# Sorted rows of 2112 bytes at a pitch of 2112, ScalarE's up parts behind the last norm, and idle transposes in TensorE's waits

## The chip, the cores and the metric

The kernel runs on one core of one Trainium2 chip. The metric is the device time of the whole kernel in microseconds (us): the median of three runs for the kernel before.

## What is computed

```python
x = x + jnp.tanh(g_xattn[0]) * _L0_xattn_ref(_layernorm(x), L0_xattn_k, fside_S2_0, ctx_2048, ctx_2048, 8)
x = x + jnp.tanh(g_ffn[0]) * _L0_ffn_ref(_layernorm(x), router_w, gate_w, up_w, down_w)
```

x is float32, 8 x 256 rows of 512. The first half is a gated long convolution: for every head (32 heads of 8 rows) the outer product kv of the normed rows and the context rows is convolved along the 512 positions with that head's filter k, a skip term is added, and the result is contracted with the context again. The second half is a mixture of experts with top-1 routing over 8 experts:

```python
routing_indices = jnp.argmax(einsum(hidden, router_w), axis=-1)
for e in range(8):
    y = (silu(hidden @ gate_w[e]) * (hidden @ up_w[e])) @ down_w[e]
    out = out + where(routing_indices == e, y, 0)
```

gate_w and up_w are 512 x 1024 for each expert, down_w is 1024 x 512.

## The kernel before, in words

The five engines and the DMA queues are programmed by hand in one block each; there is no scheduler. Every engine runs its own instructions in the order in which its block writes them, and semaphores (`wait_ge`, `then_inc`) tie them together. SyncE (SP) issues nearly all loads and stores, ScalarE (ACT) issues the loads of `xs`, and GpSimd (POOL) issues the indirect transfers.

**Attention part.** 16 groups g of 128 rows, two heads each. `stages` runs one stage per group on each engine, the middle ones in a loop. In a stage TensorE (PE) runs the convolution of group g (`conv`, 60 matmuls of 128x512 in float32r, each product taken as high times high, low times high and high times low part), the transposes of the normed rows of group g+2 (`v_in`), and for group g-1 the sum over heads (`sum_heads`) and the transposes of the second norm (`x2_in`), and for group g-2 the router's logits. VectorE (DVE) makes kv (`outer`, L962), multiplies the convolution's banks (`product`, L977), and does the residual and both norms' statistics. ScalarE takes the roots and norms and makes `kv_hi`; GpSimd makes `kv_lo` and adds products. SyncE also fills the DRAM tensor `sorted_x` in advance with rows that belong to nobody (`fill_rows`, 14 DMAs of 384 rows, written from a 128-row tile `fill`).

At the start TensorE transposes groups 0 and 1 (`v_in(0)`, `v_in(1)`), then begins stage 0. `v_in(1)` writes the bank from which VectorE makes the two products kv of group 0, so it waits for both (`s_kv`). VectorE waits for the two gates' tanh (ScalarE, L856 and L857) before its own stage 0.

**Hand-over.** Each token's normed row of 512 floats, and its number as the 513th, stands in `xn_all` in SBUF, group after group, 513 floats each. As soon as the places of groups 0 to 13 are known (`places_first`, semaphore `s_pos`), GpSimd writes those rows to their places in `sorted_x`, sorted by expert, with one indirect DMA of 128 rows per group (`scatter`, L431). The last two groups follow when the last norm, the last logits and `places_last` are done. A row of `sorted_x` is 513 floats, 2052 bytes, and so is its pitch. Meanwhile the first expert's weights are loaded in chunks of 512 KB through the one buffer `raw` (four chunks per matrix, L441) and split into high and low parts: for gate and up of expert 0 ScalarE makes the high part (`first_high_parts`, L456) and VectorE the low part (`first_low_parts`, L463). A chunk of up is loaded when the same chunk of gate has been split, a chunk of down when the same chunk of up has been. In ScalarE's order, the first two chunks of up stand ahead of the last group's root and norm (`root2(G - 1)`, L811 and L768):

```python
                xn2T_out(G - 2)
                logits_out(G - 2)
                act.wait_ge(s_y, G * 2 * LB)
                first_high_parts(act, UP, range(2))
                root2(G - 1)
                norm2(G - 1, 1)
```

**Expert part.** When all 16 scatters have landed (`s_scat`), ScalarE loads a tile of 128 sorted rows into `xs` (L878), TensorE transposes it (`x_in_array`, L1208), ScalarE and GpSimd make its high and low parts (L882, L884, L712), and TensorE runs gate and up (`project`, L1219, 24 matmuls each), the transposes of the next `xs`, `down` of the tile before (L1232, 24 matmuls) and the transposes of `hid` (L1252). In this run there are 19 such tiles, then `down` of the last tile alone, and its rows go out with an indirect DMA (L724). All later weights are split by VectorE alone (L1078, L1081). Tiles 0 and 1 belong to expert 0.

Of the kernel before, what the change touches and what calls it, by code (L numbers as in the profile page):

```python
# [5 lines left out]
def flamingo_layer_kernel(  # L6
# [30 lines left out]
    f32 = mybir.dt.float32  # L37
# [24 lines left out]
    KPAD = P + L  # L62
    CH = 4
# [6 lines left out]
    sorted_x = nc.dram_tensor("sorted_x", [FILL * (G - 2) * P, L + 1], f32)  # L70
# [6 lines left out]
    def put(name, shape, dt=f32, at=None):  # L77
        size = 4
        for n in shape[1:]:
            size *= n  # L80
        size = (size + 31) // 32 * 32
        if at is None:
            at = place
        t = nc.alloc_sbuf_tensor_at(name, shape, dt, offset=at[0])
        at[0] += size
        return t
# [37 lines left out]
    place[0] += 4 * G  # L124
# [26 lines left out]
    xn_all = put("xn_all", [P, G, L + 1], f32, [up_at + slot])  # L151
# [8 lines left out]
    assert up_at + slot + 4 * G * (L + 1) <= down_at  # L160
# [35 lines left out]
    fill = put("fill", [P, L + 1], f32, att)  # L196
# [7 lines left out]
    with ctx:  # L204
# [95 lines left out]
        def known(g, test):  # L300

            return test(g) if isinstance(g, int) else True
# [125 lines left out]
        def scatter(eng, groups):  # L428

            for g in groups:  # L430
                nc.gpsimd.indirect_dma_start(  # L431
                    out=sorted_x[:, :], out_offset=bass.IndirectOffsetOnAxis(ap=pos[:, g:g + 1], axis=0),
                    in_=xn_all[:, g, :], in_offset=None).then_inc(s_scat, 16)
# [73 lines left out]
        with nc.Block() as block:  # L507

            @block.sync
            def _(eng):  # L510
# [26 lines left out]
                def fill_rows(g):  # L537
                    eng.dma_start(sorted_x[blk(g - 1, FILL * P), :].rearrange("(k p) n -> p k n", p=P),
                                  fill[:, :].unsqueeze(1).broadcast_to([P, FILL, L + 1])).then_inc(s_zfill, 16)
# [62 lines left out]
            def _(eng):  # L602
                nc.gpsimd.memset(fill[:, 0:L], 0.0).then_inc(s_const, 1)
                nc.gpsimd.memset(fill[:, L:L + 1], float(NOBODY)).then_inc(s_const, 1)
# [24 lines left out]
                nc.gpsimd.memset(hot[:, G1:G + 1, :], 0.0).then_inc(s_const, 1)  # L629

# [64 lines left out]
                eng.wait_ge(s_xnc, G1)  # L695
# [66 lines left out]
            def _(act):  # L762
# [98 lines left out]
                act.wait_ge(s_y, G * 2 * LB)  # L861
                first_high_parts(act, UP, range(2))
# [6 lines left out]
                first_high_parts(act, UP, range(2, CH))  # L869

                def load(t):
                    if isinstance(t, int) and t == 0:
                        place = slice(0, P)
                    else:
                        act.wait_ge(s_next, t)
                        place = bass.ds(act.value_load(tile_at[0:1, blk(t)], min_val=0,
                                                       max_val=(FILL * (G - 2) - 1) * P), P)
                    act.dma_start(xs[:, :], sorted_x[place, :]).then_inc(s_xs, 16)  # L878
# [42 lines left out]
            def _(dve):  # L921
# [145 lines left out]
                first_low_parts(dve, UP, range(2))  # L1067
# [3 lines left out]
                first_low_parts(dve, UP, range(2, CH))  # L1071
# [36 lines left out]
            def _(pe):  # L1108
                def transposes(bank, src, done):
                    for b in range(LB):  # L1110
                        last = nc.tensor.transpose(bank[:, b * P:(b + 1) * P], src(slice(b * P, (b + 1) * P)),  # L1111
                                                   ident[:, :])
                    last.then_inc(done, 1)

# [56 lines left out]
                def stage(g, u, n):  # L1171
                    before = known(g, lambda g: g >= 1)
                    conv(g, u, n, 0, (0, 1, 2))
                    if known(g, lambda g: g >= 2):
                        logits_of(g - 2)
# [15 lines left out]
                v_in(1)  # L1191
# [63 lines left out]

                x_in_array(0)
                pe.wait_ge(s_tab, 1)
                last_tile = tiles(pe, tile)
                down(last_tile)
# [39 lines left out]
```

## Time and profile before

| what | value |
|---|---|
| median of 3 runs | 741.34 us (739.51 to 743.07) |
| the profiled execution's own time | 740.68 us |
| its span, first to last instruction | 738.8 us |
| busy: PE / DVE / ACT / POOL | 87% / 68% / 33% / 76% of the span |
| mean granted clock of TensorE | 0.938 of full speed |
| chain that ended last | PE 78%, DMA 7%, POOL 6%, DVE 4% |
| DMA | 117.8 MB, mean 159 GB/s |

PE, DVE, ACT and POOL stand for TensorE, VectorE, ScalarE and GpSimd. The span leaves out some 2 us ahead of and behind the instructions. The chain is followed back from the last instruction, at each step to what released it. The clock is what the chip granted TensorE: 1.00 is 2.4 GHz, 0.50 is 1.2 GHz. For the start of the program, up to 21.5 us, the trace holds no clock, and 1.00 is shown there.

### The profile page before, as it was taken

The numbers are of one execution on the slowest core, as the hardware profiler recorded it, in microseconds if no ns is written. First come the engines' busy times: TensorE is split into PE (matmuls) and PEld (weight loads), VectorE is DVE, ScalarE is ACT, GpSimd is POOL, SyncE is SP. The second block draws the span as 40 slices with busy tenths as digits, with TensorE's granted clock in tenths as the row PEclk, the third lists the DMA queues.
The fourth block names the chain that finished last, engine by engine and source line by source line (L and its number), as shares of the span: only waits on it lengthen the run. The fifth ranks groups of instructions, "written<-read, shape, count | busy, mean of one in ns | idle before, by whom it ended". The sixth has DMA issues, their size and how long they took to land.

```text
span 738.8 us, 10659 instructions
## 1 busy us (share of the span) xinstructions
PE 639.8 (87%) x3058; PEld 524.0 (71%) x3059; DVE 499.7 (68%) x631; ACT 241.7 (33%) x351; POOL 559.7 (76%) x361
## 2 busy tenths in 40 slices
PE   0989999999999999310379999999999999999964
PEld 0878888888888878310258888888888888888853
DVE  5678888888888897650746557599999938533200
ACT  4534333344334432220022332323333333333330
POOL 2799999999999998630224777798888878786852
PEclk9999999999999999655589999999999999999996
DMA  7156778677777763799864444466665655431110
GB/s 228 61 144 174 183 186 207 177 171 183 194 189 174 181 163 139 140 151 109 249 219 128 155 156 156 154 197 213 223 213 202 217 157 183 142 130 28 56 43 4
DMA packets 52031, 117.80 MB, mean 159 GB/s; under 512 B 5772, under 2 KB 5964, under 8 KB 52016
## 3 DMA queue, kind: packets, MB, share of 16 engines
q1 hardware_dynamic: 43712, 99.35, 49.0%
q0 software_dynamic: 4320, 12.60, 7.5%
q10 hardware_dynamic: 3984, 5.67, 2.7%
q8 instruction: 7, 0.11, 0.1%
q14 instruction: 8, 0.07, 0.0%
HBM read 94.60 MB, written 24.57 MB: 161 GB/s over the span
## 4 chain that ended last, share of the span: by engine, by line
PE 78%; DMA 7%; POOL 6%; DVE 4%; issue 3%; ACT 2%; SPq 0%; POOLq 0%; DVEq 0%; ACTq 0%
PE pair L1219 30%; PE bank L1131 23%; PE bank L1232 15%; DMA sorted_x<-xn_all,pos 4%; PE pair L1161 3%; POOL kv_lo L648 2%; PE bank L1252 2%; PE pair L1111 2%; POOL prod L665 2%; DMA raw<-up_w 2%; PE pair L1142 2%; PE bank L1208 1%; DVE kv L962 1%; ACT kv_hi L794 1%; DMA xs<-sorted_x 1%
## 5 line engine op out<-in xcount | busy, mean ns | idle before, releaser
L1131 PE MATMUL bank<-kv_hi,strip 128*128 128x512 f32 x640 | 213.6, 403 | 0.1
L648 POOL TENSOR_TENSOR kv_lo<-kv,kv_hi 128x2048 fp32r<-128x2048 f32 x31 | 144.1, 4649 | 3.9 <-ACT kv_hi L794 3.9
L1131 PEld LDWEIGHTS bank<-kv_hi,strip 128*128 128x128 f32 x640 | 121.6, 190 | 26.8 <-issue 0.8
L1131 PE MATMUL bank<-kv_lo,strip 128*128 128x512 f32 x320 | 126.4, 395 | 0.0
L1219 PE MATMUL pair<-gate,xT_hi 128*128 (+1 forms) x304 | 101.6, 416 | 5.5 <-issue 5.5
L977 DVE TENSOR_TENSOR prod<-bank,cT 128x512 f32<-128x512 f32 x128 | 85.2, 683 | 28.4 <-PE bank L1131 24.5
L794 ACT ACTIVATE kv_hi<-kv 128x2048 fp32r<-128x2048 f32 x32 | 61.4, 1919 | 119.8 <-DVE kv L962 110.2
L1219 PE MATMUL pair<-up,xT_hi 128*128 (+1 forms) x304 | 95.8, 396 | 0.0
L734 POOL TENSOR_TENSOR hid<-hid,mid 128x1024 f32<-128x1024 f32 x19 | 49.7, 2614 | 42.5 <-ACT mid L897 42.4
L1078 DVE CAST down_hi<-raw 128x1024 fp32r<-128x1024 f32 x32 | 31.0, 969 | 70.0 <-PE bank L1232 53.3
L962 DVE TENSOR_TENSOR kv<-pair,cK 128x2048 f32<-128x2048 f32 x32 | 72.9, 2279 | 0.4 <-PE pair L1111 0.4
L1219 PEld LDWEIGHTS pair<-gate,xT_hi 128*128 128x128 f32 x304 | 58.6, 198 | 19.4 <-issue 6.1
L1131 PEld LDWEIGHTS bank<-kv_lo,strip 128*128 128x128 f32 x320 | 60.9, 190 | 12.2
L665 POOL TENSOR_TENSOR prod<-prod 128x2048 f32<-128x2048 f32 x15 | 69.0, 4597 | 0.1
L1232 PE MATMUL bank<-down_hi,hT_hi 128*128 128x512 f32 x152 | 62.7, 412 | 5.7 <-POOL hT_lo L739 5.7
L1219 PEld LDWEIGHTS pair<-up,xT_hi 128*128 128x128 f32 x304 | 57.3, 188 | 14.0
L1219 PE MATMUL pair<-gate,xT_lo 128*128 (+1 forms) x152 | 62.2, 409 | 0.0
L712 POOL TENSOR_TENSOR xT_lo<-xT_raw,xT_hi 128x512 fp32r<-128x512 f32 x20 | 32.8, 1640 | 37.5 <-ACT xT_raw L884 37.5
L1232 PE MATMUL bank<-down_lo,hT_hi 128*128 128x512 f32 x152 | 61.0, 401 | 0.0
L1232 PE MATMUL bank<-down_hi,hT_lo 128*128 128x512 f32 x152 | 60.8, 400 | 0.0
L1219 PE MATMUL pair<-up,xT_lo 128*128 (+1 forms) x152 | 60.2, 396 | 0.0
L1081 DVE TENSOR_TENSOR down_lo<-raw,down_hi 128x1024 fp32r<-128x1024 f32 x32 | 55.8, 1745 | 1.1
(142 smaller groups left out, 1078.0 us busy)
## 6 DMA issues: line engine op xcount, KB each, us to landing
strip<-kparts SPq DMA_DIRECT2D x16, 1024.0 KB, 6.0
raw<-gate_w SPq DMA_DIRECT2D x32, 512.0 KB, 4.0
raw<-up_w SPq DMA_DIRECT2D x32, 512.0 KB, 4.3
raw<-down_w SPq DMA_DIRECT2D x32, 512.0 KB, 3.7
sorted_x<-fill SPq DMA_DIRECT2D x14, 769.5 KB, 8.5
xs<-sorted_x ACTq DMA_DIRECT2D x21, 256.5 KB, 2.7
x_in<-x_back SPq DMA_DIRECT2D x16, 256.0 KB, 7.8
cK<-ctx_back SPq DMA_DIRECT2D x16, 256.0 KB, 7.8
```

The costliest lines, as they stand in the source:

```text
L648: nc.gpsimd.tensor_tensor(kv_lo[u][:, hh, :], kv[:, hh, :], kv_hi[u][:, hh, :].bitcast(f32), ALU.subtract).then_inc(s_klo, 1)
L665: nc.gpsimd.tensor_tensor(prod[u][:, 0:J // 2, :], prod[u][:, 0:J // 2, :], prod[u][:, J // 2:J, :], ALU.add).then_inc(s_add, 1)
L712: nc.gpsimd.tensor_tensor(flat(xT_lo), xT_raw[:, :], flat(xT_hi).bitcast(f32), ALU.subtract)\
L734: nc.gpsimd.tensor_tensor(hid[:, :], hid[:, :], mid[:, :], ALU.mult).then_inc(s_hid, 1)
L794: nc.scalar.activation(kv_hi[u][:, hh, :], kv[:, hh, :], ACT.Copy).then_inc(s_khi, 1)
L962: nc.vector.tensor_tensor(kv[:, hh, :].rearrange("p (a i j) -> p a i j", i=J, j=J), v.unsqueeze(3).broadcast_to([P, LB * NB, J, J]), c.uns ...
L977: nc.vector.tensor_tensor(dst[:, :, :, hh * J:(hh + 1) * J], y_bank[lb][:, :].rearrange("p (b i j) -> p b i j", i=J, j=J), c, ALU.mult).th ...
L1078: nc.vector.tensor_copy(hi, raw[:, c, :]).then_inc(s_whi, 1)
L1081: nc.vector.tensor_tensor(lo, raw[:, c, :], hi.bitcast(f32), ALU.subtract)\
L1131: last = nc.tensor.matmul(y_bank[lb][:, :], strip[u][:, 2 * hh + t, d * P:(d + 1) * P], v[u][:, hh, mb * COL:(mb + 1) * COL], start=(mb == ...
L1219: last = nc.tensor.matmul(bank[:, half * 512:(half + 1) * 512], a[:, b, :], weights[:, bass.ds(o, 512)], start=(b == 0 and n == 0), stop=( ...
L1232: last = nc.tensor.matmul(out_bank[:, :], a[:, b, :], w[:, b * 512:(b + 1) * 512], start=(b == 0 and n == 0), stop=(b == IB - 1 and n == 2))
```

## The change

It has three parts, and nothing else moves.

1. A row of `sorted_x` becomes 528 floats, 2112 bytes, and so does its pitch. The scatter reads 528 floats from a group's place in SBUF, that is its own 513 and the first 15 of the next group's (behind the last group stand 15 more, set to zero), so GpSimd's first scatters wait for one more group's rows (`G1 + 1`). The load of `xs` still takes 513 floats of each row. The filled rows grow in the same way.
2. On ScalarE all four high parts of up stand behind the last norm, the last logits and the load of Silu's table; on VectorE all four low parts of up stand behind the tile table.
3. On TensorE `v_in(1)` moves from the head of the program into stage 0, behind the first three blocks of the convolution. Where TensorE waits, transposes of `ident` into a bank that nobody reads are put: 40 behind `v_in(0)`, 80 ahead of the first `x_in_array`, 16 behind it, and 36 ahead of the last `down`.

The diff, without the lines that only rename or assert:

```diff
+    ROW = L + 16
-    sorted_x = nc.dram_tensor("sorted_x", [FILL * (G - 2) * P, L + 1], f32)
+    sorted_x = nc.dram_tensor("sorted_x", [FILL * (G - 2) * P, ROW], f32)
...
-    place[0] += 4 * G
+    place[0] += (4 * (G + ROW - L) + 31) // 32 * 32
...
-    xn_all = put("xn_all", [P, G, L + 1], f32, [up_at + slot])
+    xn_rows = put("xn_rows", [P, G * (L + 1) + ROW - L - 1], f32, [up_at + slot])
+    xn_all = xn_rows[:, 0:G * (L + 1)].rearrange("p (g n) -> p g n", n=L + 1)
...
-    fill = put("fill", [P, L + 1], f32, att)
+    fill = put("fill", [P, ROW], f32, att)
...
-                    in_=xn_all[:, g, :], in_offset=None).then_inc(s_scat, 16)
+                    in_=xn_rows[:, g * (L + 1):g * (L + 1) + ROW], in_offset=None).then_inc(s_scat, 16)
...
-                                  fill[:, :].unsqueeze(1).broadcast_to([P, FILL, L + 1])).then_inc(s_zfill, 16)
+                                  fill[:, :].unsqueeze(1).broadcast_to([P, FILL, ROW])).then_inc(s_zfill, 16)
...
-                nc.gpsimd.memset(fill[:, L:L + 1], float(NOBODY)).then_inc(s_const, 1)
+                nc.gpsimd.memset(fill[:, L:ROW], float(NOBODY)).then_inc(s_const, 1)
...
+                nc.gpsimd.memset(xn_rows[:, G * (L + 1):], 0.0).then_inc(s_const, 1)
...
-                eng.wait_ge(s_xnc, G1)
+                eng.wait_ge(s_xnc, G1 + 1)
...
-                act.wait_ge(s_y, G * 2 * LB)
-                first_high_parts(act, UP, range(2))
                 root2(G - 1)
                 norm2(G - 1, 1)
                 xn2T_out(G - 1)
                 xn2_out(G - 1, 1)
                 logits_out(G - 1)
                 nc.scalar.activation(mark_act[:, :], ones[:, 0:1], ACT.Silu)
-                first_high_parts(act, UP, range(2, CH))
+                act.wait_ge(s_y, G * 2 * LB)
+                first_high_parts(act, UP, range(CH))
...
-                    act.dma_start(xs[:, :], sorted_x[place, :]).then_inc(s_xs, 16)
+                    act.dma_start(xs[:, :], sorted_x[place, 0:L + 1]).then_inc(s_xs, 16)
...
                 first_low_parts(dve, GATE, range(3, CH))
-                first_low_parts(dve, UP, range(2))
                 pick_experts(dve, 1, G1, G)
                 places_last(dve)
                 tile_table(dve)
-                first_low_parts(dve, UP, range(2, CH))
+                first_low_parts(dve, UP, range(CH))
...
+                def keep_busy(n):
+
+                    for _ in range(n):
+                        nc.tensor.transpose(y_bank[3][:, 0:P], ident[:, :], ident[:, :])
...
                     conv(g, u, n, 0, (0, 1, 2))
+                    if isinstance(g, int) and g == 0:
+                        v_in(1)
...
                 v_in(0)
-                v_in(1)
+                keep_busy(40)
                 stages(pe, stage)
...
+                keep_busy(80)
                 x_in_array(0)
+                keep_busy(16)
                 pe.wait_ge(s_tab, 1)
                 last_tile = tiles(pe, tile)
+                for _ in range(36):
+                    nc.tensor.transpose(gate_bank[:, 0:P], ident[:, :], ident[:, :])
                 down(last_tile)
```

The next rows show what stands in a row on an engine, for three places. ScalarE around the last group's norm, before (up<-raw are the high parts of up, sd is the root, xn_135 the normed rows, mark_act the load of Silu's table):

```order
L800 ACTIVATE logits<-pair 128x8
L456 ACTIVATE up<-raw 128x1024 x2
L811 ACTIVATE sd_76<-ve_75 128x1
L768 ACTIVATE xn_135<-x_res,nb_78,rs_77 128x512
L816 ACTIVATE xn2T<-pair 128x512
L783 ACTIVATE xn_all<-xn_135 128x512
L800 ACTIVATE logits<-pair 128x8
L868 ACT_TABLE_LOAD
L868 ACTIVATE mark_act<-ones 128x1
L456 ACTIVATE up<-raw 128x1024 x2
L878 DMA xs<-sorted_x 128x513
```

and after:

```order
L803 ACTIVATE logits<-pair 128x8
L814 ACTIVATE sd_76<-ve_75 128x1
L771 ACTIVATE xn_135<-x_res,nb_78,rs_77 128x512
L819 ACTIVATE xn2T<-pair 128x512
L786 ACTIVATE xn_rows<-xn_135 128x512
L803 ACTIVATE logits<-pair 128x8
L869 ACT_TABLE_LOAD
L869 ACTIVATE mark_act<-ones 128x1
L458 ACTIVATE up<-raw 128x1024 x4
L880 DMA xs<-sorted_x 128x513
```

The root is no longer behind two parts of up; all four now stand between the table's load and the first load of `xs`.

TensorE from the last logits to the first tile, before (xs is the tile of sorted rows, hot the one-hot routing):

```order
L1142 MATMUL pair<-router,xn2T 128x8 x4
L356 MATMUL pair<-hot,upper_b 128x24
L359 MATMUL pair<-hot,ones_b 128x16
L359 MATMUL pair<-hot,ones_b 128x8
L1208 MATMUL bank<-ident,xs 128x128 x4
L1219 MATMUL pair<-gate,xT_hi 128x512 x2
```

and after:

```order
L1148 MATMUL pair<-router,xn2T 128x8 x4
L358 MATMUL pair<-hot,upper_b 128x24
L361 MATMUL pair<-hot,ones_b 128x16
L361 MATMUL pair<-hot,ones_b 128x8
L1119 MATMUL bank<-ident 128x128 x80
L1216 MATMUL bank<-ident,xs 128x128 x4
L1119 MATMUL bank<-ident 128x128 x16
L1227 MATMUL pair<-gate,xT_hi 128x512 x2
```

The four transposes of `xs` now stand behind 80 idle ones, and the first tile behind 16 more.

TensorE at the head of the program, before (the first eight transposes are groups 0 and 1, then comes the convolution of group 0):

```order
L1111 MATMUL pair<-ident,xn 128x128 x8
L1131 MATMUL bank<-kv_hi_98,strip_105 128x512
L1131 MATMUL bank<-kv_lo_100,strip_105 128x512
L1131 MATMUL bank<-kv_hi_98,strip_105 128x512 x2
L1131 MATMUL bank<-kv_lo_100,strip_105 128x512
```

and after:

```order
L1112 MATMUL pair<-ident,xn 128x128 x4
L1119 MATMUL bank<-ident 128x128 x40
L1137 MATMUL bank<-kv_hi_98,strip_105 128x512
L1137 MATMUL bank<-kv_lo_100,strip_105 128x512
L1137 MATMUL bank<-kv_hi_98,strip_105 128x512 x2
```

Group 1's four transposes have left this place (they stand 18 matmuls further on), and 40 idle ones have come in.

## Rows read from the trace of the kernel before

**Rows 1.** page, part 2: granted clock in tenths, 40 slices of the span

```profile
PEclk9999999999999999655589999999999999999996
```

**Rows 2.** chain that ended last: start us, us, what

```profile
322.65 32.19 DMA sorted_x<-xn_all,pos
354.87 4.37 DMA xs<-sorted_x
359.28 1.11 PE bank L1208 x4
360.39 3.49 issue
363.88 14.29 PE pair L1219 x48
...
384.88 14.06 PE pair L1219 x48
...
405.85 11.25 PE pair L1219 x48
...
423.13 0.88 PE bank L1252 x8
...
708.05 5.61 PE bank L1232 x24
...
717.76 2.36 POOL hT_lo L739
...
720.24 8.06 PE bank L1232 x24
```

**Rows 3.** stretches: us, PE PEld DVE ACT POOL busy, PEclk, DMA share, GB/s

```profile
304.00:305.00 1.00, 0.71 (x4) 0.71 (x5) 1.00 (x2) 0.00 (x0) 0.88 (x1) 0.50 0.96 377
...
306.00:322.00 16.00, 4.35 (x21) 3.36 (x19) 7.97 (x23) 4.84 (x9) 10.58 (x10) 0.50 1.08 130
```

**Rows 4.** DMA view of 120 to 140 us, 40 slices of 0.5 us

```profile
GB/s 82 107 147 176 234 184 152 98 25 37 102 213 233 135 242 356 406 397 397 115 0 0 41 139 262 402 402 345 160 172 94 160 201 152 193 127 217 246 201 143
```

**Rows 5.** DMA issues by line: KB each, median us to landing

```profile
xs<-sorted_x ACTq DMA_DIRECT2D x21, 256.5 KB, 2.7
...
out<-ys,id_rows POOLq DMA_INDIRECT x19, 4.6
```

**Rows 6.** timeline around the last norm and the scatters: start us, us

```profile
308.94 0.15 DVE L930 TENSOR_SCALAR ve<-mv 128x1 f32<-128x1 f32 x1
...
312.55 1.06 ACT L456 ACTIVATE up<-raw 128x1024 fp32r<-128x1024 f32 x1 [6.45 <-DMA raw<-up_w]
...
313.51 0.19 ACT L811 ACTIVATE sd<-ve 128x1 f32<-128x1 f32 x1
...
315.19 2.35 DVE L463 TENSOR_TENSOR up<-raw,up 128x1024 fp32r<-128x1024 f32 x2
...
316.42 1.97 POOL L431 DMA_INDIRECT sorted_x<-xn_all,pos  x1 [0.30 <-issue]
...
321.38 0.97 POOL L431 DMA_INDIRECT sorted_x<-xn_all,pos  x1 [2.99 <-DVE pos L397]
...
324.86 0.15 DVE L426 CAST tile_q<-tq_f 1x23 int32<-1x23 f32 x1
```

**Rows 7.** stretches with the clock, and a timeline row of twelve transposes

```profile
44.90:48.80 3.90, 3.88 (x17) 3.46 (x18) 3.75 (x6) 1.71 (x1) 3.90 (x2) 0.62 0.44 126
...
363.80:369.60 5.80, 5.72 (x14) 4.50 (x15) 5.70 (x7) 0.00 (x0) 1.76 (x2) 0.50 0.77 230
...
304.29 2.82 PE L1161 MATMUL pair<-ident,prod 128*128 128x128 f32 x12 [3.78 <-DVE prod L1007]
```

**Rows 8.** timeline of the first convolution

```profile
18.09 1.09 PE L1111 MATMUL pair<-ident,xn 128*128 128x128 f32 x4 [8.94 <-DVE kv L962]
...
21.53 0.69 DVE L977 TENSOR_TENSOR prod<-bank,cT 128x512 f32<-128x512 f32 x1 [3.59 <-ACT tanh_f L857]
...
22.62 0.69 DVE L977 TENSOR_TENSOR prod<-bank,cT 128x512 f32<-128x512 f32 x1 [0.40 <-PE bank L1131]
```

More of the change, by code:

```diff
@@ L159, in flamingo_layer_kernel @@
     assert half[0][0] <= down_at + slot and half[1][0] <= up_at
-    assert up_at + slot + 4 * G * (L + 1) <= down_at
+    assert up_at + slot + 4 * (G * (L + 1) + ROW - L - 1) <= down_at
     table = [down_at + 4 * (J + 1) * LB * P]
```

## The prediction

> **What bounds the kernel now.** Read first the clock of TensorE over the span [rows 1]: it is full everywhere except for four slices just before the middle, where the engine has next to nothing to do. Then the chain that ended last [rows 2]. In the two long stages it runs through TensorE: a tile of the expert part has 11.25 us of gate and up, 5.6 of down and 0.9 of transposes, one behind the other. Between the stages it leaves TensorE: from 322.65 us it waits 32.19 us for the last scatter to land, then 4.37 for xs, 1.11 for its transposes, 3.49 until the parts of xs are made, and the first tile's gate and up begin at 363.88. They take 14.29 us instead of 11.25, since the clock is still half. The end leaves TensorE once more: the last down waits until 720.24 for its operand from GpSimd and takes 8.06 instead of 5.61.
>
> Why do 32 us pass? Look at bytes per second against the DMA engines' busy share [rows 3]. Both stretches are full (0.96 and 1.08), but one moves 377 GB/s and the other 130. The scatters are 16 times 128 rows of 2052 bytes, 4.2 MB, and the first of them ran fast. So the engines are not short of work, their packets are held up, and that begins once some hundred rows have been written. The same shape shows in the attention part, where 384 filled rows of the same pitch go to the same tensor [rows 4]: with them the rate stands at 402, 402 and 345 GB/s for 1.5 us (132 to 133.5 us) and then at 160, 172, 94. The load of the strips just before, 1 MB read and none written to DRAM, holds 356 to 406 for four slices. What is slow is a burst of writes of such rows. At 2052 bytes, two neighbouring rows share a piece of 64 bytes, and each row begins and ends inside one; at 2112 (33 times 64) none does.
>
> **The rows of 2112 bytes.** That a row costs a partial write at both ends is my reading; no row of this trace shows a long burst of aligned writes. The nearest is the scatter of the output, 128 rows of 2048 bytes, which lands 4.6 us from its issue [rows 5]. Bounds: the last scatter lands as now (no gain), or 4.6 us after its issue. I take the second, since xs, x and the output move whole rows at full rate. Bytes grow by 3%: 4.3 MB of scatter, 2.1 of up and 0.5 of x in the 24 us from the first scatter (298) to 322 need 290 GB/s, below the 377 of rows 3. The wait for one more group costs nothing: that copy ends at 296.2, 1.9 us ahead of the first scatter. The filled rows lie in the attention part's DMA time, beside a full TensorE; if that cover failed, TensorE would show waits for strip.
>
> A rule speaks against this part. The Trainium skill (DMA: Bandwidth & Descriptors, How a descriptor splits into AXI transactions) counts transactions that must start at multiples of 256 bytes; a row pitch of 2112 still puts three rows in four off such a place. By that count alone the change would win nothing here; it is the case "rate unchanged" below.
>
> **The up parts.** The last group's variance is ready at 309.09 (308.94 and 0.15), but ScalarE takes the root at 313.51, behind an up part that waited 6.45 us for its chunk [rows 6]. Now it goes at 309.25: everything up to the last places comes 4.3 us sooner. GpSimd starts the last pair of scatters at 321.38 - 4.3 = 317.1. It must be through with the first 14: at its usual 1.27 us each it is through by 316.6, instead of 318.4 (the 1.97 us of one issue [rows 6] is back-pressure). The 16th is issued at 318.4, lands at 323.0. The moved parts: ScalarE is through with Silu's table at 316.2, then 4 x 1.06 = 4.2, so 320.4, 2.6 us ahead of the landing. VectorE ends the tile table at 325.0 - 4.3 = 320.7 and needs 4 x 1.2 = 4.9 for the low parts [rows 6]: 325.6, while TensorE wants up at about 337. Down's chunks start behind those, at 322 to 325.6 in SyncE's queue; VectorE then has 12 chunks of two instructions (some 1.9 us each, 23 us), ready at about 353, and TensorE wants the third matrix set at about 370. Free, with 17 us of cover.
>
> **The load of xs** takes 2.7 us at the median [rows 5] against 4.37: 323.0 + 2.7 = 325.7, at worst 327.4.
>
> **The 80 transposes** start when the last count is done, 320.3 - 4.3 = 316.0. One costs 0.21 us at the low clock (twelve in 2.82 us [rows 7] less four in 1.11 [rows 2], over eight) and 0.11 at full clock (0.88 for eight [rows 2]). All at the low clock: 17.1 us; all at full clock: 8.8. Does the clock rise under transposes? Between 44.9 and 48.8 TensorE ran 2 us of transposes and then 1.9 of matmuls, and the clock was up at 48.8; in the first tile it stayed at 0.50 through 5.8 us of matmuls alone [rows 7]. So transposes count, and I take 5.1 us at the low clock (24 of them) and 56 at full: 6.2. They end at 327.3, 1.6 us later than xs is there: a small price, on the path. The four transposes of xs then take 0.6, and the parts 3.49 as now, under which the 16 lie (1.8 us). The first tile begins at 327.3 + 0.6 + 3.5 = 331.4: **32.5 us** sooner. It runs at full clock: 14.29 - 11.25 = **3.0**. The second tile stays slow (14.06 [rows 2]), since the wait ahead of it is as before: 0, at most 2.8.
>
> The Trainium skill says otherwise of transposes (TensorE: Matmul & The Clock Gate, Part 4: PE-mode transpose): they do not count as busy for the clock. The rise at 48.8 us speaks against it. What it would do here is the case "clock stays low".
>
> **The end.** 36 transposes are 4 us in the 5.7 us wait between 714.5 and 720.24; with the clock kept the last down takes 5.6 instead of 8.06: **2.4**. The operand is not sooner. **The start.** 40 transposes end between 14 and 18 us, about when the convolution can start (its kv_lo is there at 15.7); before, it waited for v_in(1), at 18.09 [rows 8]. But VectorE starts its products at 21.53, behind the tanh. Only its second product, which waited 0.40 us for TensorE, comes sooner: **0.3**, and v_in(1) is done before VectorE wants it.
>
> Sum: 32.5 + 3.0 + 2.4 + 0.3 = 38.2. The profiled execution took 740.7: 702.5. It lies 0.7 below the median of the runs shown, so **703 us**. A measurement of this kernel can tell about 0.5%, 3.7 us.
>
> **The rivals.**
> - *Writes still held up in part*: bursts of rows are slow also when aligned, only less so. For it: no long aligned burst is shown. If half of the 32 us stays, the last scatter lands at 339, xs at 342, TensorE is cold again, the first tile starts at 346.6 (17.3 sooner) and gains 1.5 at its clock; with 2.4 and 0.3 this is 21.5, so 720 us, and 711 to 729 for shares around a half.
> - *Rate unchanged*: the bytes of a line are not what holds the packets, and the landing stays where it is, since it goes by throughput. Left are 1.5 for the first tile (the 16 transposes warm the clock before it), 2.4 and 0.3: 4.2, so 736 to 737 us. Against it: reads of the same size run at 400.
> - *Clock stays low*: the scatters are fast but 80 transposes take 17.1 us, to 333.1; xs 1.1, parts 3.5, start at 337.7 (26.2 sooner), no gain at the first tile or the end: 715 us.
> - *Slower*: one mechanism, transposes that only occupy TensorE, with the rate unchanged. At the start 40 at 0.21 us last until 17.7, then 18 matmuls at 0.41 (5.72 us for 14 [rows 7]) come ahead of v_in(1), which ends at 26.2 instead of 19.2, past the 23.8 at which VectorE made the next kv: 2.4 later. At the end 36 at 0.21 take 7.7 from 714.5: 2.0 too late. Together 4.4: 746 us. It decides if a transpose stays above 0.16 us at the end and the scatters win under 1 us.
>
> **How the numbers follow.** Forecast 0.60, held up in part 0.15, rate unchanged 0.13, clock low 0.08, slower 0.04. The forecast's own range is 696 (second tile warm, all transposes at full clock) to 709. The range goes from there over the clock case and most of the partial one to 728: 0.79. Faster by over 0.5% (below 737.6) are the first two, the clock case and 0.08 of the unchanged one: 0.91; within 0.5% its rest and a little of the last: 0.06; slower 0.03.
>
> **What the new profile would show.** Bytes per second near 300 from 300 to 320 us; the last scatter landed at about 323; the root right behind the variance; TensorE's clock full from about 321; the first tile at 331 in 11.3 us; the last down in 5.6. A last landing beyond 330 refutes the step on the rows; a clock of 0.50 under the 80 transposes refutes the one on the clock; a wait of TensorE for parts of up, down or gate in the first three tiles refutes the cover of the moved parts.

## The result, and the profile after

| | before | after |
|---|---|---|
| time, us | 741.71 (739.51 to 743.07) | 700.89 (700.56 to 704.74) |
| profiled execution, us | 740.68 | 704.74 |
| its span, us | 738.8 | 703.0 |
| mean granted clock | 0.938 | 0.977 |

Both medians are of four executions beside each other. The ratio of after to before is 0.946, with a 95% interval of 0.943 to 0.950. 703 us were predicted, 2.1 above the median. The profiled execution of the changed kernel is the slowest of those measured; why is taken up under e8.

The chain that ended last in the changed kernel (start us, us, what; the counterpart of [rows 2]):

```profile
319.18 5.38 DMA sorted_x<-xn_rows,pos
324.58 5.19 DMA xs<-sorted_x
329.81 1.12 PE bank L1216 x4
330.93 3.41 PE bank L1119 x16
334.34 11.96 PE pair L1227 x48
...
353.02 12.96 PE pair L1227 x48
...
372.90 11.21 PE pair L1227 x48
...
684.08 2.36 POOL hT_lo L742
686.56 5.87 PE bank L1240 x24
```

The 32.19 us of the scatter are 5.38 now. The first tile starts 29.5 us sooner (334.34 for 363.88) and takes 2.3 less (11.96 for 14.29), the second takes 1.1 less (12.96 for 14.06), the last down 2.2 less (5.87 for 8.06). These are 35.1 of the 35.8 us by which the span shrank.

Stretches of the changed kernel (us, busy PE PEld DVE ACT POOL, PEclk, DMA share, GB/s; the counterpart of [rows 3]):

```profile
304.00:305.00 1.00, 0.00 (x0) 0.00 (x0) 1.00 (x2) 0.00 (x0) 0.70 (x2) 1.00 1.06 392
...
306.00:322.00 16.00, 10.45 (x66) 9.71 (x65) 9.64 (x37) 7.59 (x11) 11.59 (x12) 0.71 0.95 335
```

And its DMA view of 120 to 140 us, where two fills of 384 rows lie, 40 slices of 0.5 us (the counterpart of [rows 4]):

```profile
GB/s 348 369 143 37 29 8 0 0 0 0 82 156 229 168 184 287 397 410 406 279 25 0 0 131 111 384 418 414 376 211 286 410 410 402 168 0 0 0 0 0
```

In the same 16 us (306 to 322) 335 GB/s move where 130 did, with the DMA engines as full as before (share 0.95, before 1.08). A fill runs at 376 to 418, where before it fell to 94 to 172, and lands 4.7 us from its issue (the median of 14) instead of 8.5. In those 16 us the engines served 1696 packets, before 617. So each packet is served faster, and what held them up goes with the writes of these rows.

The clock, and the 80 idle transposes (stretches, then a timeline row of TensorE: start us, us):

```profile
314.00:318.00 4.00, 2.70 (x16) 2.60 (x16) 2.39 (x14) 3.29 (x5) 3.01 (x4) 0.50 0.89 346
318.00:320.00 2.00, 2.00 (x16) 2.00 (x16) 1.80 (x7) 2.00 (x3) 1.70 (x2) 0.79 1.01 397
320.00:322.00 2.00, 2.00 (x20) 2.00 (x19) 1.93 (x9) 0.16 (x1) 0.82 (x2) 1.00 0.82 310
...
328.00:330.00 2.00, 0.19 (x1) 0.19 (x2) 1.97 (x3) 0.00 (x0) 0.00 (x0) 0.77 1.04 364
330.00:332.00 2.00, 2.00 (x10) 2.00 (x10) 1.97 (x3) 1.03 (x2) 0.00 (x0) 0.50 1.01 387
332.00:336.00 4.00, 4.00 (x16) 3.61 (x16) 3.93 (x4) 0.06 (x1) 2.92 (x3) 0.51 0.84 265
```

```profile
316.05 10.27 PE L1119 MATMUL bank<-ident 128*128 128x128 f32 x80
329.81 1.12 PE L1216 MATMUL bank<-ident,xs 128*128 128x128 f32 x4 [3.49 <-DMA xs<-sorted_x]
```

The clock rises from 0.50 to 1.00 while TensorE does nothing but transposes. In this execution they end at 326.3, and xs comes at 329.8: TensorE waits 3.49 us, the clock is back at 0.50, and the 16 transposes behind those of xs run at the low clock. The chain puts them on the path with 3.41 us. That is not their price, since GpSimd makes xT_lo, the low part of the tile, at the same time:

```profile
332.23 1.26 POOL L715 TENSOR_TENSOR xT_lo<-xT_raw,xT_hi 128x512 fp32r<-128x512 f32 x1 [11.41 <-ACT xT_raw L886]
333.46 1.17 POOL L719 TENSOR_TENSOR id_next<-xs,ones 128x1 f32<-128x1 f32 x1
334.00 1.20 PE L1227 MATMUL pair<-gate,xT_hi 128*128 128x512 f32 x2
```

The first tile starts 0.5 us behind GpSimd's next instruction here, and 0.1 in the kernels without these transposes (e1, e3). So they cost some 0.4 us. The trace of before could not show this second cold stretch.

### The profile page after: what moved, and what is told of

Read it like the earlier page. It is cut to its first block, busy times and chain, and to the rows that moved or that the text cites. A ratio compares the mean times of both kernels' runs of the same rounds, so it can differ in the third digit from the quotient of the medians.

```text
span 703.0 us, 11004 instructions
## 1 busy us (share of the span) xinstructions
PE 656.1 (93%) x3230; PEld 541.6 (77%) x3231; DVE 504.4 (72%) x631; ACT 241.4 (34%) x351; POOL 553.9 (79%) x362
## 4 chain that ended last, share of the span: by engine, by line
PE 77%; DVE 8%; POOL 6%; DMA 3%; issue 3%; ACT 2%; SPq 0%; DVEq 0%; POOLq 0%; ACTq 0%
PE pair L1227 31%; PE bank L1137 21%; PE bank L1240 15%; PE pair L1167 3%; POOL kv_lo L651 2%; PE bank L1260 2%; DVE prod L1009 2%; DVE kv L964 2%; POOL prod L668 2%; PE pair L1112 2%; PE bank L1216 1%; ACT kv_hi L797 1%; DMA x_dram<-x_res 1%; PE pair L1148 1%; DVE prod L979 1%
## 5 line engine op out<-in xcount | busy, mean ns | idle before, releaser
L1227 PE MATMUL pair<-gate,xT_hi 128*128 (+1 forms) x304 | 99.1, 407 | 1.2 <-issue 1.2
L1227 PEld LDWEIGHTS pair<-gate,xT_hi 128*128 128x128 f32 x304 | 57.0, 193 | 14.0 <-issue 1.6
L725 POOL TENSOR_TENSOR ys<-ys,x2s 128x512 f32<-128x512 f32 x19 | 34.1, 1792 | 23.7 <-ACT ys L892 23.6
```

Source lines behind the costliest of these rows:

```text
L725: nc.gpsimd.tensor_tensor(ys[:, :], ys[:, :], x2s[:, :], ALU.add).then_inc(s_yadd, 1)
L1227: last = nc.tensor.matmul(bank[:, half * 512:(half + 1) * 512], a[:, b, :], weights[:, bass.ds(o, 512)], start=(b == 0 and n == 0), stop=( ...
```

## The experiments

Each kernel is the changed one with the edit shown, except e1. The median of before beside them was 740.75 us for e1 to e4, 741.88 for e5 to e8 and 741.79 for e9 to e12. Differences from the changed kernel are against its 700.89, which was measured with another group of runs. For e3 and e4 the ratios to before are 0.948 (0.941 to 0.956) and 0.949 (0.941 to 0.957) and overlap with the 0.946 (0.943 to 0.950) of the changed kernel. Their differences of under 4 us therefore lean on what the traces show beside the times.

### The parts one by one

**e1, rows alone:** the kernel before with part 1 of the change only.

```diff
+    ROW = L + 16
-    sorted_x = nc.dram_tensor("sorted_x", [FILL * (G - 2) * P, L + 1], f32)
+    sorted_x = nc.dram_tensor("sorted_x", [FILL * (G - 2) * P, ROW], f32)
...
-                eng.wait_ge(s_xnc, G1)
+                eng.wait_ge(s_xnc, G1 + 1)
```

> The kernel before with rows and pitch of 2112 bytes alone. If whole aligned rows are what frees the writes: scatters at 350 GB/s or more, and since the chunks of up land early too, ScalarE's root is not held up either; last scatter landed at about 324, first tile at about 333 at the low clock (14.3 us), last down 8.1 us: 706 to 711 us. If the rows do nothing and the gain is the order of the parts and the clock: 741 us.

Measured: 711.51 us (709.63 to 712.81), ratio 0.958 (0.950 to 0.966). The rows alone bring 29 us of the 41. The time lies just above the expected 706 to 711: xs took 6.49 us from 325.27, and the first tile starts at 335.58.

**e2, all but the rows:**

```diff
-    ROW = L + 16
+    ROW = L + 1
...
-                nc.gpsimd.memset(xn_rows[:, G * (L + 1):], 0.0).then_inc(s_const, 1)
...
-                eng.wait_ge(s_xnc, G1 + 1)
+                eng.wait_ge(s_xnc, G1)
```

> The changed kernel with rows and pitch back at 2052 bytes; the parts of up and the transposes as changed. If the rows carry the gain: the last scatter lands near 355 us as before and 736 us remain (2.4 from the last down, 1.5 from the first tile, 0.3 from the start). If the rows do nothing: 701 us.

Measured: 736.07 us (734.91 to 737.00, ten executions), ratio 0.992 (0.989 to 0.995). This is the 736 to 737 that the prediction worked out for "rate unchanged". The chain of e2:

```profile
318.18 39.11 DMA sorted_x<-xn_rows,pos
357.31 4.26 DMA xs<-sorted_x
...
366.14 11.41 PE pair L1226 x48
...
718.05 5.87 PE bank L1239 x24
```

The last scatter is issued sooner than before (318.18 for 322.65) and still lands only at 357.3: the landing goes by throughput. 4.7 us remain of the other two parts.

That the sum came out is in part luck: the landing is 2.5 us later than before (357.3 for 354.8), and the first tile starts 2.3 later. But that tile takes 11.41 us instead of 14.29, a gain of 2.9 where 1.5 were forecast, the second takes 12.97 instead of 14.06, and the last down gains 2.2. The 80 transposes had ended 34.95 us before xs came. So the 16 behind xs alone brought the clock up, and they did it at no price: from the start of xs's transposes to the first tile it is 4.5 us, before it was 4.6.

**e3, no idle transposes:** `keep_busy(40)`, `keep_busy(80)`, `keep_busy(16)` and the 36 ahead of the last down are taken out.

```diff
-                keep_busy(40)
...
-                keep_busy(80)
...
-                keep_busy(16)
...
-                for _ in range(36):
-                    nc.tensor.transpose(gate_bank[:, 0:P], ident[:, :], ident[:, :])
```

> The changed kernel without any of the 172 idle transposes (group 1's v stays behind the first three blocks). If the transposes win only what the clock gives in the last down and the first tile: last down 8.1 instead of 5.9, first tile 14.3 instead of 12.3 us, less 0.7 for the 16 that end on the path: 704 to 706 us. If they only occupy TensorE: 700 us or less.

Measured: 704.51 us (704.16 to 706.51), 3.6 us above the changed kernel. The chain of e3:

```profile
318.74 3.59 DMA sorted_x<-xn_rows,pos
322.35 4.17 DMA xs<-sorted_x
326.57 1.11 PE bank L1215 x4
327.68 2.89 issue
330.57 13.84 PE pair L1226 x48
...
685.80 8.14 PE bank L1239 x24
```

First tile 13.84 and last down 8.14, both begun at the low clock: 11.96 and 5.87 with the transposes, which is 4.2 us. (This profiled execution took 706.51, 2 us above the median of e3, so the agreement with 3.6 is rough.) At the start nothing is lost: VectorE's next kv begins at 23.48 without the 40 transposes, at 23.39 with them.

**e4, two up parts ahead again:**

```diff
+                act.wait_ge(s_y, G * 2 * LB)
+                first_high_parts(act, UP, range(2))
                 root2(G - 1)
...
-                first_high_parts(act, UP, range(CH))
+                first_high_parts(act, UP, range(2, CH))
...
                 first_low_parts(dve, GATE, range(3, CH))
+                first_low_parts(dve, UP, range(2))
                 pick_experts(dve, 1, G1, G)
...
-                first_low_parts(dve, UP, range(CH))
+                first_low_parts(dve, UP, range(2, CH))
```

> The changed kernel with the first two parts of up ahead of the last norm again, on ScalarE and VectorE. If the root was held up only because the chunk of up was stuck behind the scatters (landing after 11.5 us), it now lands within 5 us and the root goes at 309.9 as in the changed kernel: 701 us, no difference. If the order itself is worth 4.3 us, as the prediction's step has it: 705 us.

Measured: 704.74 us (704.18 to 705.58), 3.8 above the changed kernel. So by the times the order of the up parts counts, but not by the way that the prediction gave. The timeline of e4 (start us, us; in brackets the idle time before and what ended it):

```profile
305.79 1.06 ACT L458 ACTIVATE up<-raw 128x1024 fp32r<-128x1024 f32 x1 [1.57 <-DMA raw<-up_w]
308.42 0.20 ACT L814 ACTIVATE sd<-ve 128x1 f32<-128x1 f32 x1 [1.57 <-DVE ve L933]
...
311.68 11.30 SPq L443 DMA_DIRECT2D raw<-down_w  x4
```

With fast rows the chunk of up is there early, and the root waits for its variance alone, with two parts ahead of it. What differs is SyncE's queue: chunks of down go out from 311.68, while in the changed kernel they start at 322.08, behind the last scatter's issue. In e4 xs took 6.17 us from 324.16, and came 4.03 us after TensorE was through with the 80 transposes. Whether down's chunks delay it is what e8 tests, below.

### The rows: alignment, length or pitch

**e5, e6, e7, other pitches:** the theory of the prediction, partial writes at both ends of a row, against the count of 256-byte pieces and against the pitch.

```diff
-    ROW = L + 16
+    ROW = L + 8
```

(2080 bytes, e5; `L + 17`, 2116 bytes, in e6; `L + 64`, 2304 bytes, in e7.)

> The changed kernel with rows and pitch of 2080 bytes, 65 times 32: every row starts and ends at a multiple of 32 bytes, every second one not at a multiple of 64. If pieces of 64 bytes decide: slow writes again, last scatter landed near 340 to 355 us, 720 to 736 us. If 32 bytes are enough: 701 us, as with 2112.

> The changed kernel with rows and pitch of 2116 bytes, 4 bytes longer than 2112. If it is the place of a row's ends that decides: the scatters are held up as at 2052, 736 us. If a longer row or another spread over the memory did it: 701 us.

> The changed kernel with rows and pitch of 2304 bytes, 9 times 256. By the count of transactions that start at multiples of 256 bytes, this pitch should be the one that wins, over 2112 as well: below 700 us. If multiples of 64 are enough, the bytes grow by 9% for nothing: 701 to 703 us.

Measured: e5 699.86 us (698.80 to 700.40), e6 701.95 (698.58 to 708.23), e7 702.17 (700.58 to 702.96). By their medians all three are as fast as 2112 bytes; why one execution of e6 took 708.23 stays open.

**e9, the filled rows short:** 2052 bytes written at a pitch of 2112, in the fills only.

```diff
-                    eng.dma_start(sorted_x[blk(g - 1, FILL * P), :].rearrange("(k p) n -> p k n", p=P),
-                                  fill[:, :].unsqueeze(1).broadcast_to([P, FILL, ROW])).then_inc(s_zfill, 16)
+                    eng.dma_start(sorted_x[blk(g - 1, FILL * P), 0:L + 1].rearrange("(k p) n -> p k n", p=P),
+                                  fill[:, 0:L + 1].unsqueeze(1).broadcast_to([P, FILL, L + 1])).then_inc(s_zfill, 16)
```

> The changed kernel, but the filled rows write 513 of the 528 floats of a row: length 2052, pitch 2112; the scatters stay as they are. The landing of a fill was 8.5 us at length and pitch 2052 and 4.7 at 2112. If the length is what is slow (2048 bytes and a rest of 4), the fills land in about 8 us and their burst falls below 200 GB/s; if the pitch is, they land in about 4.7 and the burst stays near 400. The whole time stays at 701 either way.

Measured: the fills land in 5.0 us; 703.76 us (two executions, 701.74 and 705.78, where 701 was expected; the slower one has no profile).

**e10, a pitch of 2064:** `ROW = L + 4`.

```diff
-    ROW = L + 16
+    ROW = L + 4
```

> The changed kernel with rows of 516 floats, length and pitch 2064: a multiple of 16 bytes. If a pitch slows the more the nearer it lies to 2048, the last scatter lands between the 5 us of 2080 and the 39 of 2052, and the time is between 705 and 730. If it is the rest of 4 bytes behind 2048, or the lack of a multiple of 16, the time is 700 as with 2080.

Measured: 702.87 us (701.45 to 705.18), ratio 0.948 (0.946 to 0.950). Fast: the 705 to 730 of a grading towards 2048 did not come. The profiled execution, the slowest, had xs late (below).

**e11, short rows at a pitch of 4104:** 513 floats each, in scatters and fills; the places are multiplied by two. The fills have the edit of e9.

```diff
-    sorted_x = nc.dram_tensor("sorted_x", [FILL * (G - 2) * P, ROW], f32)
+    sorted_x = nc.dram_tensor("sorted_x", [FILL * (G - 2) * P, 2 * (L + 1)], f32)
...
-                    out=sorted_x[:, :], out_offset=bass.IndirectOffsetOnAxis(ap=pos[:, g:g + 1], axis=0),
-                    in_=xn_rows[:, g * (L + 1):g * (L + 1) + ROW], in_offset=None).then_inc(s_scat, 16)
+                    out=sorted_x[:, :].rearrange("n (h l) -> (n h) l", h=2), out_offset=bass.IndirectOffsetOnAxis(ap=pos[:, g:g + 1], axis=0),
+                    in_=xn_rows[:, g * (L + 1):(g + 1) * (L + 1)], in_offset=None).then_inc(s_scat, 16)
...
-            V.tensor_copy(pos[:, 0:G1], pos_f[:, 0:G1]).then_inc(s_pos, 1)
+            V.tensor_scalar(pos[:, 0:G1], pos_f[:, 0:G1], 2.0, None, ALU.mult).then_inc(s_pos, 1)
```

> Rows of 513 floats (2052 bytes) at a pitch of 4104, in the scatters and the fills; no row touches the next. If the length of 2052 is what is slow, or rows whose ends fall near a multiple of 2048, it is as slow as at a pitch of 2052: fills 8 us, last scatter some 39, 736 us. If it is that neighbouring rows touch, or that they lie densely at nearly 2048, it is fast: 701.

Measured: 730.68 us (730.37 and 731.00), ratio 0.986 (0.983 to 0.988). Slow. Its chain:

```profile
317.50 32.80 DMA sorted_x<-xn_rows,pos
350.33 3.56 DMA xs<-sorted_x
```

The seven pitches side by side. The row of the page's DMA issues for the fills is (KB, median us to landing); for e2, e6, e9, e10 and e11 it reads, in this order, one fence for each:

```profile
sorted_x<-fill SPq DMA_DIRECT2D x14, 769.5 KB, 8.6
```

```profile
sorted_x<-fill SPq DMA_DIRECT2D x14, 793.5 KB, 5.4
```

```profile
sorted_x<-fill SPq DMA_DIRECT2D x14, 769.5 KB, 5.0
```

```profile
sorted_x<-fill SPq DMA_DIRECT2D x14, 774.0 KB, 5.2
```

```profile
sorted_x<-fill SPq DMA_DIRECT2D x14, 769.5 KB, 8.0
```

| length / pitch of the filled rows | run | fill lands, us | GB/s, 306 to 322 us | time, us |
|---|---|---|---|---|
| 2052 / 2052 | e2 | 8.6 | 123 | 736.07 |
| 2052 / 4104 | e11 | 8.0 | 162 | 730.68 |
| 2052 / 2112 | e9 | 5.0 | (scatters of 2112) | 703.76 |
| 2064 / 2064 | e10 | 5.2 | 305 | 702.87 |
| 2080 / 2080 | e5 | 4.7 | 311 | 699.86 |
| 2112 / 2112 | after | 4.7 | 335 | 700.89 |
| 2116 / 2116 | e6 | 5.4 | 301 | 701.95 |
| 2304 / 2304 | e7 | 4.8 | 336 | 702.17 |

What follows, one cause after the other:

- *A row that begins and ends inside a piece of 64 bytes* is not it. At 2116 each row but one in sixteen does so, as at 2052, and neighbours share a piece in both; 5.4 us and 8.6.
- *The count of 256-byte pieces* is not it. A row lies in nine of them at each of these pitches, slow or fast (at 2116 one row in four in ten). Nor is the start of a row: at 2304 every row begins at a multiple of 256, at 2112 one in four; 4.8 and 4.7.
- *The length of 2052* is not it: the same 2052 bytes land in 5.0 us at a pitch of 2112 and in 8.0 at 4104 (e9, e11).
- *Rows that touch* are not it: at 4104 there are 2052 free bytes between them.

What the two slow pitches have in common is that they lie 4 and 8 bytes above a multiple of 2048. Counted from the last multiple of 2048, the start of a row moves by only 4 or 8 bytes to the next; at 2064 by 16, at 2080 by 32, and those are fast. So the partly written ends of many consecutive rows lie at nearly the same place of that grid. That they then wait for one another in one part of the memory fits all eight cases, but it is a reading and is not shown: no run varied the order of the rows, or used a pitch just below 2048, 2048 itself, or a slow one that is not a multiple of 2052, and the traces show nothing of the memory behind the DMA engines. Shown is which pitches are slow; why they are stays open.

### Who competes, and a better version

**e8, down later:** the first load of down waits for xs.

```diff
+                eng.wait_ge(s_xs, 16)
                 load_matrix(eng, DOWN, 0, UP, 0)
```

> The changed kernel, but SyncE waits for the first xs before it loads down of expert 0. If these loads are what makes the last scatter land after 5.4 us instead of 3.6 and xs after 5.2 instead of 2.7 (as the order of the up parts suggests): xs is there at 325 to 326, and with the 80 transposes ending at 326.3 the first tile starts at 330 at full clock, in every execution: 698 to 699 us. If the loads do not matter: 701 us.

Measured: 700.60 us (699.96 to 702.12), the same as the changed kernel. xs was early, as expected, but the 80 transposes took 11.80 us here and held the path, so the 698 to 699 of that branch did not come. In its timeline xs ends no wait:

```profile
315.36 11.80 PE L1120 MATMUL bank<-ident 128*128 128x128 f32 x80
327.00 0.60 PE L1217 MATMUL bank<-ident,xs 128*128 128x128 f32 x4
327.44 1.91 PE L1120 MATMUL bank<-ident 128*128 128x128 f32 x16
330.44 0.71 PE L1228 MATMUL pair<-gate,xT_hi 128*128 128x512 f32 x2 [1.09 <-issue]
```

This is the first tile as it starts when xs is in time: 330.44. In the profiled execution of the changed kernel it started at 334.00 on the same timeline, 3.6 us later, and that execution took 704.74 where its others took 700.56 to 701.86. So two outcomes lie some 3.6 us apart, by whether xs comes before the transposes end or well behind them. e5, e6, e7 and e9, with first tiles between 329.58 and 330.95 in their profiles, took 699.9 to 702.7 us there; e4 and e10, with 334.3, took 704.9 and 705.2. The 3.8 us of e4 are of this size, and e4 took them in all four executions, e8 in none.

That xs takes longer beside chunks of weights is shown: with down held back it took 2.9 us at most in e8 (324.90 less 322.05) and 2.53 in e12, and with chunks in the queues 3.8 to 6.5 in the nine other profiles with fast rows (the changed kernel, e1, e3 to e7, e9, e10). These are chunks of down in the new order; in e4 and e1 down is nearly through by then, and chunks of expert 1's gate go out beside xs (from 324.16 and 325.12). That the old order of the up parts makes xs later still is supported (6.49 in e1, 6.17 in e4), but not shown: in e10 xs took 6.06 us with the changed kernel's order. Nor do the times tell e8 from the changed kernel, which had such an execution once in five.

**e12, down later, 66 transposes, 2080 bytes:**

```diff
-    ROW = L + 16
+    ROW = L + 8
...
+                eng.wait_ge(s_xs, 16)
                 load_matrix(eng, DOWN, 0, UP, 0)
...
-                keep_busy(80)
+                keep_busy(66)
```

> The changed kernel with rows of 2080 bytes, the first chunk of down loaded behind xs (as in e8), and 66 idle transposes ahead of xs instead of 80. With down later xs is there before the 80 transposes end (327.2 us); 14 fewer at 0.11 us are 1.5 us, so TensorE is free at 325.6, about when xs is there. Expected 699.0, that is 1 to 2 us under the changed kernel. If the clock needs the 80, it falls again in the first tile and the time is 702.

Measured: 698.95 us (698.44 to 701.12, five executions), ratio to before 0.944 (0.942 to 0.946). This is 1.9 us under the changed kernel, with intervals that overlap, so it is not shown to be better. Part of the 1.9 may be the rows of 2080 bytes, with which e5 took 699.86. Its timeline, then the waits of TensorE from 330 to 460 us (waited for: us in total, times, longest), first of e12, then of e8:

```profile
316.26 9.21 PE L1120 MATMUL bank<-ident 128*128 128x128 f32 x66
325.30 0.63 PE L1217 MATMUL bank<-ident,xs 128*128 128x128 f32 x4
...
328.59 0.70 PE L1228 MATMUL pair<-gate,xT_hi 128*128 128x512 f32 x2 [0.91 <-issue]
```

```profile
PE bank L1261 <- POOL hid L738: 4.0, 1, 4.0
PE pair L1228 <- DVE gate L1083: 1.1, 1, 1.1
```

```profile
PE bank L1261 <- POOL hid L738: 3.2, 1, 3.2
PE pair L1228 <- POOL xT_lo L716: 1.2, 1, 1.2
```

66 suffice for the clock. The first tile starts 1.9 us before that of e8, and 0.8 of it is lost ahead of the second tile: TensorE waits 4.0 us for hid instead of 3.2, since GpSimd's instruction took 3.19 us instead of 2.34. The wait behind it is as long in both. In e8 it ends with xT_lo, in e12 with a part of gate that VectorE has just split, so with down's chunks later the splits no longer lie in cover here.

**What was not tried: the 16 without the 80.** In the five profiles where the clock was low again when xs came, its transposes took 1.11 or 1.12 us and the 16 ran behind them. The first tile then took 11.41 us (e2), 11.29 (e4), 11.57 (e10), 11.64 (e11) and 11.96 (the changed kernel), against 11.45 in e8, where the clock was full all along. Without any it took 13.80 (e1) and 13.84 (e3). So most of what the idle transposes bring to the first tile comes from the 16. By these rows the 80 give some 0.5 us for the transposes of xs at the full clock and up to 0.4 for the 16, and where xs is early they hold the path: xs was there by 324.9 in e8, and TensorE took it up at 327.00. Whether the kernel would be as fast without them no run shows.

## Why the prediction was right, and where it was not

- **The size of the rows' step** held. The last scatter landed at 324.6 (predicted 323.0), after 5.4 us (4.6). In e3 and e8 it landed at 322.3 and 322.0. Bytes per second were 335, predicted "near 300". The last scatter was issued at 319.18, predicted 318.4; it followed GpSimd's own 14 scatters, as the prediction said, since its places were ready at 317.0.
- **The cause of the rows' step was wrong.** "A row costs a partial write at both ends" failed: 2116 bytes is fast (e6). The bound that I took, the landing of a scatter of whole rows, was right for a reason that the theory did not hold, and that is luck: the theory chose 2112 bytes, and every pitch tried from 2064 on would have done. The rule beside it, the count of AXI transactions (the Trainium skill, DMA: Bandwidth & Descriptors, How a descriptor splits into AXI transactions), would have kept the old rate at 2112, which did not come. By that count, an estimate from that section, a row costs nine transactions at 2052, at 2112 and at 2304, so it tells none of them apart; the expectation of e7, that 2304 should win, did not follow from it. Both ideas looked at one row by itself. The same 2052 bytes are fast at one pitch and slow at another (e9, e2), and the place of a row within 64 bytes does not sort them (e6), so what counts is how the rows lie to one another.
- **"Everything up to the last places comes 4.3 us sooner"** was right in size and wrong in cause. The root came at 309.87 instead of 313.51, 3.6 sooner. But in e1 it came at 309.47 with the old order: before, ScalarE was behind an up part that waited 6.45 us for its chunk [rows 6], and that chunk was late because of the slow rows. I took a wait that the first part of the change removes and booked it to the second. The order's 3.8 us (e4) go another way, perhaps by keeping down's chunks out of the DMA queues until the last scatter is issued; that is not shown.
- **xs** was predicted at 2.7 us, "at worst 327.4". It took 5.19 and came at 329.8 in the profiled execution. The median of 21 loads was the wrong row: this one runs beside two chunks of 512 KB of down, issued at 322.08. With those held back it took 2.5 and at most 2.9 (e12, e8). The row of the same load, 4.37 [rows 2], was the better one. In the profiles of e5, e6, e7 and e9 this cost 0 to 1.3 us of waiting, since the transposes hold the path until 325.7 to 326.3, about as the prediction had it ("they end at 327.3").
- **The 80 transposes**: predicted 11.3 us, measured 10.27 (11.80 in e8), with the clock at 0.79 from 318 to 320 and at 1.00 from 320 on, where 321 was predicted. The Trainium skill (TensorE: Matmul & The Clock Gate, Part 4: PE-mode transpose) says that transposes do not count as busy for the clock. The trace disagrees for these of 128x128 float32: from 316.05 to 326.3 TensorE ran nothing else. The argument from [rows 7] was weaker than its conclusion. It set a rise after 3.9 us with transposes against none in 5.8 us of matmuls alone. But under the same transposes the mean clock from 320 to 322 was 1.00 here and 0.68 in e8, and in the trace of before the clock rose under matmuls alone right behind those 5.8 us (0.90 from 369.6 to 372). Two rises that lie 2 us apart could not decide it.
- **First tile** at full clock: 3.0 predicted. It came to 2.3 in the profiled execution and to 2.7 to 3.0 in those of e4 to e10. **Second tile:** between 0 and 2.8 was allowed and 0 taken; it was 1.1 here. That is no gain to book to the change: with the same 80 and 16 transposes and fast rows this tile took 12.96 to 14.30 us (e7), and 13.49 without them (e3).
- **The last down**: 2.4 predicted, 2.2 measured, 5.87 us instead of 5.6. **The start**: 0.3 predicted, 0.4 measured (the first sum over heads at 44.50 for 44.91); e3 shows that the move of v_in(1) brought it and not the 40 transposes.
- **No wait for parts** of up, down or gate appeared in the first tiles of the changed kernel; the cover of the moved parts held.
- **The rivals.** "Rate unchanged" did not come; its sum was right for e2, with terms of other sizes (see there). "Slower" needed transposes above 0.16 us at the end; 36 took 4.14 us in e12, 0.115 each.

The forecast was within 2.1 us because its large term was read from a landing that a fast row shows, whatever its reason. Against the 38.2 us of its sum the profiled execution gained 35.9, with xs late, and the others 38.8 to 40.1. Of the parts, the rows bring 29 us alone. The others bring 11 on top of them and 5 without them: with fast rows they also bring the first tile 5.1 us forward (335.58 in e1, 330.44 in e8), while with slow rows the landing of the last scatter sets its start.

## What to carry to other kernels

If a burst of DMA writes shows a full busy share at a third of the bytes per second, look at the pitch of the rows in DRAM before counting bytes: rows of 2052 bytes cost some 30 us here, and 12 bytes more took them away. When one part of a change removes a wait, work out the other parts from the times that then hold, not from the trace of before. And idle transposes paid best where TensorE waits anyway for another engine behind its operand: the 16 under the making of xs's parts brought the clock up even after 35 us of rest (e2), for 0 to 0.4 us. The 80 ahead of the operand were lost when it came 3.5 us behind them, since the clock had fallen again, and held the path when it came early.

## What the runs showed of the hardware

- With rows of 2052 bytes at pitches of 2052 and 4104 the 16 us of scatters ran at 123 and 162 GB/s, with the DMA share above 1; with rows of 2064 to 2304 bytes at 301 to 336. I had expected a grading with alignment; from 2064 on there is none that the times can tell. The fills hint at a small one: 5.0 to 5.4 us for rows of 2052 bytes at 2112, of 2064 and of 2116, and 4.7 to 4.8 for 2080, 2112 and 2304.
- A slow burst of writes also holds up reads beside it: in e2 the four chunks of up took 24.1 us at the median from issue to landing, in the changed kernel 5.3. The two rows are from the DMA view of 296 to 324 us, first of e2, then of the changed kernel:

```profile
raw<-up_w SPq DMA_DIRECT2D x4, 512.0 KB, 24.1
```

```profile
raw<-up_w SPq DMA_DIRECT2D x4, 512.0 KB, 5.3
```

- Ahead of the second tile TensorE waits 3.2 us for hid, and the clock falls again (0.50 from 350 to 356 us): the changed kernel's second tile took 12.96 us and e3's 13.49, against 11.21 of the third. The idle transposes of this change do not reach that wait; filling it was not tried.
